# One 128-edge tile per lap, instead of two, takes its source columns from on-chip memory; the iota row moves from PSUM to SBUF

## The reference, cut to what matters

```
msg_in     = concat([nodes[src], nodes[dst], edge_features])       # 200000 x (64 + 64 + 32)
messages   = relu(msg_in @ mW1 + mb1) @ mW2 + mb2                  # hidden 128, output 64
aggregated = segment_sum(messages, dst, 12500)
upd        = relu(concat([nodes, aggregated]) @ uW1 + ub1) @ uW2 + ub2
out        = layernorm(nodes + upd)                                # over the 64 features
```

## Time and profile before

| what | value |
|---|---|
| median of three executions | 1916.37 us |
| the profiled execution's own time | 1918.05 us |
| its span, first to last instruction | 1916.2 us |
| POOL busy | 1394.6 us (73%) |
| PE busy, PE weight loads | 1433.5 us (75%), 1297.2 us (68%) |
| DVE busy | 1281.8 us (67%) |
| ACT busy | 1103.8 us (58%) |
| mean granted TensorE clock | 0.822 of full speed |

### The profile page before, as it was taken

One profiled execution on the slowest core, in us unless ns is written; L12 is line 12 of the kernel. 1 busy time (PEld: TensorE's weight loads), 2 busy tenths in 40 slices (PEclk: granted clock), 3 DMA queues, 4 the chain that ended last, 5 costly groups with the idle time before them and its releaser, 6 DMA issues.

```text
span 1916.2 us, 48882 instructions
## 1 busy us (share of the span) xinstructions
PE 1433.5 (75%) x10272; PEld 1297.2 (68%) x10272; DVE 1281.8 (67%) x7986; ACT 1103.8 (58%) x7125; POOL 1394.6 (73%) x1480
## 2 busy tenths in 40 slices
PE   6787777777787777767777777777877787777776
PEld 6676666667676666666676676666766677677674
DVE  3586666666666666666666777777777777777774
ACT  3485555555555555556555566665666566665652
POOL 1677777777777777777777777777777777777773
PEclk8898878777877777788778888888888887878877
DMA  9833323323322333233332323332333323233321
GB/s 210 254 100 82 83 75 84 83 79 79 86 79 77 84 82 81 80 80 81 80 80 77 81 78 82 82 83 80 80 80 82 82 79 82 79 81 82 82 80 42
DMA packets 172073, 168.28 MB, mean 88 GB/s; under 512 B 71210, under 2 KB 135186, under 8 KB 171938
## 3 DMA queue, kind: packets, MB, share of 16 engines
q0 software_dynamic: 46944, 96.24, 19.2%
q1 hardware_dynamic: 111394, 64.34, 12.1%
q10 hardware_dynamic: 13698, 7.28, 1.7%
HBM read 151.34 MB, written 16.36 MB: 88 GB/s over the span
## 4 chain that ended last, share of the span: by engine, by line
POOL 70%; issue 23%; DMA 3%; PE 1%; POOLq 1%; DVE 1%; ACT 0%; SPq 0%; DVEq 0%; ACTq 0%
POOL ag L314 70%; DMA dst_table<-picks 1%; DMA src_table<-ag 1%; DMA xc<-x_t 1%; POOLq L233 1%; PE bank L477 1%; POOLq L311 0%; DMA ag<-src_table,slot_idx 0%; DMA own_columns<-resid 0%; PE bank L353 0%; PE bank L749 0%; PE bank L755 0%; DVE picks L498 0%; DVE hid L416 0%; DMA picks<-edge_t 0%
## 5 line engine op out<-in xcount | busy, mean ns | idle before, releaser
L314 POOL DMA_INDIRECT ag<-src_table,slot_idx x1467 | 1388.0, 946 | 495.6 <-issue 446.3
L368 PE MATMUL bank<-oh,hid 128*128 128x96 f32 x3128 | 523.1, 322 | 244.1 <-DVE xc L434 231.3
L368 PEld LDWEIGHTS bank<-oh,hid 128*128 128x128 f32 x3128 | 476.3, 233 | 289.7 <-ACT hid L394 253.0
L302 ACT ACTIVATE own_x<-xc 64x4 uint8 x6144 | 627.0, 190 | 0.2
L353 PE MATMUL bank<-picked,picks 128*128 128x128 f32 x3128 | 554.8, 333 | 9.6 <-DMA picks<-edge_t 6.8
L416 DVE TENSOR_TENSOR hid<-bank,ag 128x512 f32<-128x512 f32 (+1 forms) x391 | 256.8, 657 | 442.0 <-DMA ag<-src_table,slot_idx 415.6
L394 ACT ACTIVATE hid<-hid 128x512 f32<-128x512 f32 x295 | 185.7, 629 | 562.8 <-DVE hid L416 562.2
L290 DVE COPY own_x<-xc 64x4 uint8 x6144 | 498.2, 192 | 12.0
L353 PEld LDWEIGHTS bank<-picked,picks 128*128 128x128 f32 x3128 | 495.4, 241 | 15.0 <-issue 11.1
L338 PE MATMUL bank<-ident_bf,oh 128*96 128x128 bf16 x1564 | 194.4, 259 | 151.5 <-DVE oh L402 150.8
L338 PEld LDWEIGHTS bank<-ident_bf,oh 128*96 128x96 bf16 x1564 | 142.1, 150 | 210.5 <-DVE oh L402 187.9
(11 more groups left out here) (62 smaller groups left out, 428.2 us busy)
## 6 DMA issues: line engine op xcount, KB each, us to landing
picks<-edge_t SPq DMA_DIRECT2D x391, 64.0 KB
ag<-src_table,slot_idx POOLq DMA_INDIRECT x1467
picked<-dst_table SPq DMA_DIRECT2D x391, 48.0 KB
src_table<-ag SPq DMA_DIRECT2D x25, 256.0 KB, 4.1
dst_table<-picks SPq DMA_DIRECT2D x17, 256.0 KB, 4.4
xc<-x_t ACTq DMA_DIRECT2D x8, 400.0 KB, 16.2
resid<-x_rows SPq DMA_DIRECT2D x24, 128.0 KB
out<-resid ACTq DMA_DIRECT2D x24, 128.0 KB
```

The source lines that it names most:

```text
L302: return nc.scalar.activation(to, of, ACT.Copy)
L314: pool.indirect_dma_start(out=ag[:, k, j * DH:(j + 1) * DH], out_offset=None, in_=src_table, in_offset=bass.IndirectOffsetOnAxis(ap=slot_i ...
L368: nc.tensor.matmul(ps_a[q][:, 0:WIN], hid[:, q, j * DH:(j + 1) * DH], oh[:, r, j * WIN:(j + 1) * WIN], start=(j == 0), stop=(j == TPG - 1))
```

## The change

Three things change.

```
-OWN_OF = (1, 0, 0, 0, 1, 0, 0, 0)
+OWN_OF = (1, 0, 0, 0, 0, 0, 0, 0)
-OWN_DVE = 16
+OWN_DVE = 8
...
+        iota = sb("iota", [P, WIN])
...
-        iota = banks[6][:, 0:WIN]
...
-            return nc.values_load_multi_w_load_instructions(
+            return list(nc.values_load_multi_w_load_instructions(
...
-            dve.tensor_copy(iota, iota_i[:, :])
+            dve.tensor_copy(iota[:, :], iota_i[:, :])
```

More of the change, by code:

```diff
@@ L281, in own_places @@
             at = k * OWN_N
-            return nc.values_load_multi_w_load_instructions(
+            return list(nc.values_load_multi_w_load_instructions(
                 own_list[0:1, at + a:at + b], engines=(et,), min_val=x_at, max_val=x_at + 4 * (N_NODES - 1),
-                skip_runtime_bounds_check_because="the address of a node's column in xc")[1]
+                skip_runtime_bounds_check_because="the address of a node's column in xc")[1])
         def own_columns(k, a, places, copy, s_done):
```

## The result

The changed kernel takes 1991.68 us (median of four, 1991.02 to 1992.42) against 1916.09 us before: a ratio of 1.0394, with a 95% interval of 1.0376 to 1.0411. It is slower by 75.6 us. The forecast was 1976 us in a range of 1971 to 2026: the direction and the range hold, but the change costs a quarter more than the 60 us that were its main term. The likeliest case's own range, 1972 to 1979 us, does not hold. The time lies in the span of the partial form (1980 to 2000 us), which had a chance of 0.08.

A forecast was written before the change was run, and what follows sets the result against it. The prediction took GpSimd's issue of gathers, about 1.25 us each, as the bound. 1916.37 us plus 60.0 for 48 more gathers minus 1 for L770, all else 0, gave 1975.5, rounded to 1976 us; range 1971 to 2026.

The forecast's parts named there:

- main term: 48 more gathers on GpSimd, one in each lap after lap 0, at 1.2497 us each: 60.0 us.
- likeliest case: GpSimd's extra gathers set the time and the one-hot costs 0: 1975.5 us, own range 1972 to 1979; chance 0.63.
- partial form: Only some one-hots delay a GpSimd gather, or by a fraction: 5 to 25 us, 1980 to 2000 us; chance 0.08.
- The bound: After the start GpSimd waits for no other engine and issues gathers at its own pace, 1.251 us a step.
- The gathers: GpSimd issues 1515 gathers instead of 1467, the 48 more at 1.2497 us each: 60.0 us.
- Copies, TensorE, SyncE: Fewer copies on VectorE and ScalarE, fewer matmuls with a new wait at k = 0, shorter `own_list` transfers: cost nothing.
- The one-hot: L402 on VectorE, 391 runs, gets its input from SBUF instead of PSUM: taken as 0, with 48.5 us kept.
- first rival: One-hots with two SBUF inputs hold up GpSimd's gathers: 48.5 us, 2024 us (2000 to 2065); chance 0.27.
- L770 itself: VectorE's L770 moves within its group; its 16 delays of gathers, about 2 us, may vanish or stay: -1 us.
- Not slower: Copies really set a gather's 946 ns or its 0.30 us gap: 1916 us or below; chance 0.02.
- The sum: Median before plus added gathers minus the L770 delays: 1916.37 + 60.0 - 1, given as 1975.5 us.

## Why the prediction was right, and where it was off

**The bound.** GpSimd's own pace sets the time: right. Every time of this study in which no two-input instruction and no late VectorE disturbs it follows from the number of gathers: 1442, 1467 and 1515 gathers gave 1885.3, 1915.1 and 1974.9 us. The slopes are 30.2 / 25 = 1.21 and 59.8 / 48 = 1.25 us, the step in the trace.

**The gathers.** 48 x 1.2497 = 60.0 us: measured alone as 59.8.

**Copies, TensorE, SyncE.** Cost nothing: right, by the same run. The wait at k = 0 appeared and was covered.

**The one-hot.** This is the step that failed. I took 0 and the change paid about 16 us (75.6 - 59.8). The range held in spite of it, because it had been widened to take in the rivals; the point that I named was 16 us too low. Two parts of this step were wrong. First, I read the earlier trace rows as an exemption for a repeated value. The trace after refutes it with the same L828:

```profile
1834.28 0.42 DVE L828 TENSOR_TENSOR resid<-resid,stat 128x256 f32 x1 [0.18 <-DVE stat L826]
1834.41 1.11 POOL L314 DMA_INDIRECT ag<-src_table,slot_idx  x1 [0.30 <-issue]
```

It ends at 1834.70, and the gather at 1835.52, 0.82 later. In the earlier trace rows L802 and L828 had begun 0.06 and 0.08 us after the gather, each behind a gap, since they wait for a VectorE result; L770 in the earlier trace rows, begun 0.09 us after its gather, stood right behind copies. These are the instructions of the trace before that stood in front of the L770, the L802 and the L828:

```profile
1045.79 0.30 DVE L290 COPY own_x<-xc 64x4 uint8 x3
...
1301.49 0.17 DVE L800 TENSOR_SCALAR stat<-stat 128x4 f32<-128x4 f32 x1
...
1881.30 0.18 DVE L826 RECIPROCAL stat<-stat 128x4 f32<-128x4 f32 x1
```

The copies end 0.08 us after L770's start (1046.09 against 1046.01). L800 and L826 end 0.04 and 0.03 us before the starts of L802 and L828. I compared their inputs and not what stood in front of them. The sentence of the Trainium skill (SBUF — State Buffer, Who interferes with whom) that I set against these two samples holds without the exception: all of 361 instructions in the table's first row held a gather up. The same section of the Trainium skill also says that a `tensor_tensor` was not seen to stall a DMA, and infers why; the prediction left this out when it called the first rival the page's forecast. For the gathers of this case the measurement decides against it, by the same 361.

Second, the rival's price of 48.5 us came from one-hots spread evenly over the gather's period. They are not. I worked out from the copies that the one-hot would come 0.6 us earlier behind L416; it came 0.9 us earlier (1.81 for 2.70 us). By the medians of 316 groups of each kernel, the copies give 0.55 us of it. Another 0.22 us lies between L416 and L433, 0.83 us in the earlier trace rows's kernel and 0.61 after, where the order shows that a register load has gone. The last 0.13 us is the iota row itself: from the last copy to the one-hot it is 0.20 us before and 0.07 after, and in the run with only the own tile, where the row is in PSUM, 0.23. In the pair of groups shown, L416 also lies 0.27 us earlier against the gathers:

```profile
1005.94 0.95 POOL L314 DMA_INDIRECT ag<-src_table,slot_idx  x1 [0.30 <-issue]
```

Before, L416 begins 0.32 us after this gather (1006.26), and after, 0.05 us after one (1002.99 against 1004.19 - 1.25 = 1002.94). At 0.6 us earlier the one-hot would have ended on the next gather's point. At 0.89 + 0.27 us earlier it ends before that gather begins. That is luck of the place, as the run with six more copies on VectorE shows.

**L770 itself.** -1 us: of no weight, and so near to it partly by chance. Before, 16 L770 held up gathers for 2.1 us. In the run with only the own tile none did, but L802 and L828 did, for 1.0 us in all.

**Not slower.** The copies don't set the gather's time: the median went from 945 to 944 ns with half of them, which is the lower bound that I gave, and it is 944 ns too in the run with three own tiles, then two, which has more copies than before.

**The sum.** 1916.37 + 60.0 - 1 is 1975.4, not 1975.5; it changes nothing.

## What to carry to other kernels

Count what the bounding engine must issue and multiply by its step: that gave three of these times to 1.5 us. A cheap-looking move of an operand can cost more than that, so look whether it makes an instruction of VectorE read two SBUF tensors while GpSimd issues DMAs, and keep one input in PSUM if so. And when two samples seem to contradict a rule, compare what came before them on their engine before you make an exception of their form.

## What the runs showed of the hardware

- A VectorE instruction with two SBUF inputs that began 0.05 to 0.45 us before a gather on GpSimd and was still running 0.14 us after its start held the gather up in 361 of 361 cases; the gather then ends 0.82 us after it. Undelayed a gather takes 0.945 us.
- Right behind another instruction, it did so in 416 of 420 cases when it began 0.05 us before to 0.175 us after the gather. Behind a gap of VectorE it did so in none of 65.
- A wait on VectorE in front of such an instruction, which opens a gap and lets it start 0.25 to 0.28 us later, made two kernels faster, by 61 and by 52 us.
- With no wait between them, a one-hot begins 0.07 us after the start of the last copy with its two inputs in SBUF, and 0.19 to 0.23 us after it with one in PSUM (medians).
- The price of the same 391 instructions was between 16 and 94 us, by their place in a period of 1.25 us.
